# Moving the rows of maxima, a query split and two stack fills to other queues and other places in a one-core decoder layer

## The reference

```python
x = x + self_attention(layernorm(x))          # 16 heads of 8, rotary, causal
x = x + cross_attention(layernorm(x), ctx)    # 16 heads of 8, keys and values from ctx, + b_proj
x = x + moe(layernorm(x))                     # mean over tokens -> 8 experts, best 2, 128 -> 512 -> 128, gelu
```

## Time and profile before

| | |
|---|---|
| runs of the kernel before | 199.74, 200.00, 201.43 us; median 200.0 |
| the profiled execution | 200.95 us; its span 199.2 us |
| mean granted TensorE clock | 0.947 of full |
| PE busy | 166.8 us (84%) |
| DVE busy | 140.7 us (71%) |
| ACT busy | 104.8 us (53%) |
| POOL busy | 52.3 us (26%) |
| DMA | 19.05 MB, mean 96 GB/s |

### The profile page before, as it was taken

One profiled execution on the slowest core, in us unless ns is written; L12 is line 12 of the kernel. 1 busy time (PEld: TensorE's weight loads), 2 busy tenths in 40 slices (PEclk: granted clock), 3 DMA queues, 4 the chain that ended last, 5 costly groups with the idle time before them and its releaser, 6 DMA issues.

```text
span 199.2 us, 4411 instructions
## 1 busy us (share of the span) xinstructions
PE 166.8 (84%) x1500; PEld 116.1 (58%) x1508; DVE 140.7 (71%) x545; ACT 104.8 (53%) x222; POOL 52.3 (26%) x103
## 2 busy tenths in 40 slices
PE   0686195699599979989998998998998899799994
PEld 0343184485466755755764655654665556598984
DVE  2789299897347899799799889888968346525020
ACT  2132021257147656566566666766676657793451
POOL 7810005668800070030030030010115107126050
PEclk9999669589769999999999999999999999999999
DMA  5817660058227503322321321300340350170720
GB/s 150 238 35 175 164 173 18 3 148 184 70 82 196 184 25 104 110 69 58 109 82 49 98 95 35 90 0 3 113 130 3 100 143 0 17 224 26 229 66 26
DMA packets 23842, 19.05 MB, mean 96 GB/s; under 512 B 2364, under 2 KB 21820, under 8 KB 23100
## 3 DMA queue, kind: packets, MB, share of 16 engines
q1 hardware_dynamic: 22908, 17.79, 31.9%
q10 hardware_dynamic: 912, 0.98, 2.0%
HBM read 12.54 MB, written 2.49 MB: 75 GB/s over the span
## 4 chain that ended last, share of the span: by engine, by line
PE 50%; DVE 19%; DMA 15%; SPq 5%; issue 4%; POOL 3%; ACT 2%; POOLq 0%; DVEq 0%; ACTq 0%
PE psV L914 11%; PE psB L893 9%; PE psA L868 8%; DMA stackQ<-maxT 6%; DMA stackQ<-scratch 4%; DVE masked L623 4%; PE psA L958 4%; PE psM L923 3%; PE psA L975 3%; DMA stackK<-hid 3%; PE psV L975 3%; PE psM L933 3%; DVE stats L554 2%; DVE negmax L629 2%; SPq L402 2%
## 5 line engine op out<-in xcount | busy, mean ns | idle before, releaser
L753 ACT ACTIVATE E<-psB 128x512 f32<-128x512 f32 x112 | 62.3, 595 | 37.3 <-PE psB L893 15.7
L868 PE MATMUL psA<-stackK,stackQ 72*128 72x256 bf16 (+1 forms) x256 | 44.4, 277 | 11.8 <-DMA stackK<-hid 5.5
L893 PE MATMUL psB<-stackQ,stackK 74*128 74x256 bf16 (+1 forms) x256 | 42.2, 264 | 4.6 <-DMA stackQ<-maxT 3.8
L623 DVE CUSTOM_DVE_ANT_0 masked<-psA,row_mask 128x128 bf16<-128x128 f32 (+1 forms) x128 | 36.8, 352 | 11.8 <-PE psA L868 11.7
L629 DVE TENSOR_REDUCE negmax<-psA 128x2 f32<-128x512 f32 x64 | 39.7, 677 | 0.0
L868 PEld LDWEIGHTS psA<-stackK,stackQ 72*128 72x128 bf16 x256 | 23.0, 105 | 21.5 <-DMA stackQ<-scratch 8.6
L914 PE MATMUL psV<-E,V 128*9 128x256 f32 (+1 forms) x512 | 30.9, 359 | 0.2 <-ACT E L753 0.2
L893 PEld LDWEIGHTS psB<-stackQ,stackK 74*128 74x128 bf16 x256 | 22.0, 100 | 12.5 <-DMA stackQ<-maxT 5.6
L468 POOL TENSOR_SCALAR rstd<-mv 128x2 f32<-128x2 f32 x12 | 2.8, 236 | 89.1 <-DVE mv L558 88.9
L914 PEld LDWEIGHTS psV<-E,V 128*9 128x9 f32 x512 | 11.0, 90 | 14.4 <-issue 7.9
L761 ACT ACTIVATE oT<-psV 128x256 f32<-128x256 f32 x32 | 12.3, 384 | 7.9 <-PE psV L914 7.2
(11 more groups left out here) (111 smaller groups left out, 247.0 us busy)
## 6 DMA issues: line engine op xcount, KB each, us to landing
stackK<-scratch SPq DMA_DIRECT2D x18, 192.0 KB
stackQ<-hid SPq DMA_DIRECT2D x36, 64.0 KB
w1s<-w_dram SPq DMA_DIRECT2D x8, 258.0 KB, 2.8
w2s<-w_dram SPq DMA_DIRECT2D x8, 256.0 KB, 3.7
stackQ<-scratch SPq DMA_DIRECT2D x3, 576.0 KB
stackK<-hid SPq DMA_DIRECT2D x18, 64.0 KB
scratch<-hid SPq DMA_DIRECT2D x4, 192.0 KB, 3.7
scratch<-parts_ctx SPq DMA_DIRECT2D x4, 192.0 KB, 4.7
```

The source lines that it names most:

```text
L623: last = dve.tensor_tensor_reduce(out=masked[:, bank, i * keys:(i + 1) * keys], in0=scores[:, i, 0:keys], in1=row_mask[:, S - keys:S], sca ...
L753: act.activation(dst, psB[:, bank].rearrange("p (h q) -> p h q", h=dst.shape[1]), ACT.Exp, scale=SCALE).then_inc(b_taken, 1)
L868: last = pe.matmul(psA[:, bank, i * keys:(i + 1) * keys], stackQ[0:ROWS, b, h, t * P:(t + 1) * P], stackK[0:ROWS, b, h, 0:keys], start=Tru ...
L893: last = pe.matmul(psB[:, bank, i * n:(i + 1) * n], stackK[:, b, h, t * P:(t + 1) * P], stackQ[:, b, h, q0:S], start=(s == 1 or i == 0), s ...
```

## The change

Four edits in one.

1. The step max_rows is split into three. max_turn (PE's transpose) and row_out (the two DMAs) stand behind the units of half 8j+8, max_rows (DVE) stands ahead of them: DVE takes the maxima before the two new units of scores. The DMAs are issued by ACT instead of SP; ACT first waits for DVE's second instruction. Only for job 0 do the three stay together, behind half 7.
2. In q_cross ACT copies the product from PSUM into a new tile qc of two buffers, and POOL splits it from there, ahead of its addition of the bias (line 495). DVE has nothing left of this step.
3. stack_write and stack_read of batches 2 and 3 become one step for the keys (last argument 1) and one for the queries (0). For batch 2: keys written behind half 6, queries behind 9, keys read behind 9, queries behind 10 (before: both written behind 9, both read behind 10). For batch 3: 13, 14, 14, 15 (before: 14, and the read behind 17).
4. The scratch output of the masked maxima has two buffers instead of three, and its wait is for DVE's own unit before last.

```diff
+    put(7, "max_turn", 0, 0)
     put(7, "max_rows", 0, 0)
+    put(7, "row_out", 0, 0)
...
-    put(9, "stack_write", 0, 2)
-    put(10, "stack_read", 0, 2)
-    put(14, "stack_write", 0, 3)
+    put(6, "stack_write", 0, 2, 1)
+    put(9, "stack_write", 0, 2, 0)
+    put(9, "stack_read", 0, 2, 1)
+    put(10, "stack_read", 0, 2, 0)
+    put(13, "stack_write", 0, 3, 1)
+    put(14, "stack_write", 0, 3, 0)
+    put(14, "stack_read", 0, 3, 1)
+    put(15, "stack_read", 0, 3, 0)
...
         if j > 0:
-            put(n + 2 * NG, "max_rows", s, b)
-        if j == 1:
-            put(n + 2 * NG + 1, "stack_read", 0, 3)
+            row_of[n + 2 * NG] = (s, b)
...
+        if half in row_of:
+            order.append(("max_rows", *row_of[half]))
         order += [step for _, step in sorted(units, key=lambda unit: unit[0])]
+        if half in row_of:
+            order += [("max_turn", *row_of[half]), ("row_out", *row_of[half])]
...
# SP
-                if kind == "stack_write" and s == 0:
-                    sp.wait_ge(parts_k_self[b], NPART)
-                    write_parts(0, b, 1, parts[:, b, 1], scr_k_self[b])
-                    sp.wait_ge(parts_q_self[b], NPART)
-                    write_parts(0, b, 0, parts[:, b, 0], scr_q_self[b])
-                if kind == "stack_read" and s == 0:
-                    sp.wait_ge(scr_k_self[b], 16)
-                    read_k(s, b)
-                    sp.wait_ge(scr_q_self[b], 16)
-                    read_q(s, b)
+                if kind == "stack_write":
+                    which = st["g"]
+                    sp.wait_ge((parts_q_self[b], parts_k_self[b])[which], NPART)
+                    write_parts(s, b, which, parts[:, b, which], (scr_q_self[b], scr_k_self[b])[which])
+                if kind == "stack_read":
+                    which = st["g"]
+                    sp.wait_ge((scr_q_self[b], scr_k_self[b])[which], 16)
+                    if which == 1:
+                        read_k(s, b)
+                    else:
+                        read_q(s, b)
...
-                if kind == "max_rows":
-                    sp.wait_ge(misc_taken[st["misc"][0][0]], st["misc"][0][1])
-                    for i in range(2):
-                        sp.dma_start(stackQ[MAXROW + i:MAXROW + i + 1, b].rearrange("o h (t q) -> o (h t) q", t=NT),
-                                     maxT[:, b, i, :]).then_inc(maxrow_in[b], 16)
...
# POOL
                 if kind == "q_cross":
+                    bank, k = misc[0]
+                    pool.wait_ge(misc_taken[bank], k)
+                    split(qc[:, b % 2], parts[:, b, 0], parts_q[b])
...
# DVE
-                if kind == "q_cross":
-                    bank, k = misc[0]
-                    dve.wait_ge(misc_full[bank], k)
-                    qq, dst = rot[:, b % 2, 0, 0], parts[:, b, 0]
-                    dve.tensor_copy(dst[:, 0], psM[:, bank, 0:S]).then_inc(parts_q[b], 1)
-                    dve.wait_ge(parts_q[b], 1)
-                    dve.tensor_tensor(qq, psM[:, bank, 0:S], dst[:, 0], ALU.subtract).then_inc(misc_taken[bank], 1)
-                    dve.wait_ge(misc_taken[bank], k)
-                    dve.tensor_copy(dst[:, 1], qq).then_inc(parts_q[b], 1)
-                    dve.wait_ge(parts_q[b], 2)
-                    dve.tensor_tensor(dst[:, 2], qq, dst[:, 1], ALU.subtract).then_inc(parts_q[b], 1)
...
-                        if unit >= NA:
-                            dve.wait_ge(a_taken, unit - NA + 1)
+                        if unit >= 2:
+                            dve.wait_ge(a_taken, unit - 1)
...
# ACT
+                if kind == "row_out":
+                    bank, k = use[("max_turn", s, b)][0]
+                    act.wait_ge(misc_taken[bank], k)
+                    for i in range(2):
+                        act.dma_start(stackQ[MAXROW + i:MAXROW + i + 1, b].rearrange("o h (t q) -> o (h t) q", t=NT),
+                                      maxT[:, b, i, :]).then_inc(maxrow_in[b], 16)
...
+                if kind == "q_cross":
+                    bank, k = misc[0]
+                    act.wait_ge(misc_full[bank], k)
+                    if b >= 2:
+                        act.wait_ge(parts_q[b - 2], NPART)
+                    act.activation(qc[:, b % 2], psM[:, bank, 0:S], ACT.Copy).then_inc(misc_taken[bank], 1)
```

More of the change, by code:

```diff
@@ L72, in plan @@
 def plan():
-    extra = {}
+    extra, row_of = {}, {}
     def put(half, *step):
@@ L161, in plan @@
     uses = {"ln_turn": 1, "v_self": 1, "ctx_turn": 1, "k_cross": 1, "v_cross": 1, "q_cross": 1,
-            "max_rows": 1, "o_turn": 2, "o_back": 1, "o_proj": 1, "route": 1}
+            "max_turn": 1, "o_turn": 2, "o_back": 1, "o_proj": 1, "route": 1}
     count, total, steps = [0, 0], 0, []
@@ L226, in build @@
         row_mask = sb("row_mask", [P, S])
-        masked = sb("masked", [P, NA, 2 * S], BF16)
+        masked = sb("masked", [P, 2, 2 * S], BF16)
         mask16T = sb("mask16T", [P, GH, P], BF16)
@@ L239, in build @@
         kc = sb("kc", [P, NB, S])
+        qc = sb("qc", [P, 2, S])
         hid = sb("hid", [P, NHID, NC, S])
@@ L619, in _ @@
                             dve.wait_ge(row_mask_set, 1)
-                        if unit >= NA:
-                            dve.wait_ge(a_taken, unit - NA + 1)
+                        if unit >= 2:
+                            dve.wait_ge(a_taken, unit - 1)
                         for i in range(nh):
-                            last = dve.tensor_tensor_reduce(out=masked[:, bank, i * keys:(i + 1) * keys], in0=scores[:, i, 0:keys],
+                            last = dve.tensor_tensor_reduce(out=masked[:, unit % 2, i * keys:(i + 1) * keys], in0=scores[:, i, 0:keys],
                                                             in1=row_mask[:, S - keys:S], scale=-1.0, scalar=LARGEST,
@@ L870, in _ @@
                     last.then_inc(a_full, 1)
-                if kind == "max_rows":
+                if kind == "max_turn":
                     pe.wait_ge(a_taken, a_units_until(job))
```

## The result

| | before | after |
|---|---|---|
| median of 11 runs | 200.27 us (199.4 to 203.2) | 203.74 us (201.7 to 205.3) |
| ratio | | 1.0138, interval 1.0087 to 1.019 |
| profiled execution, span | 200.95, 199.2 us | 202.06, 200.3 us |
| mean granted clock in it | 0.947 | 0.940 |

The kernel became 1.4% slower, clear of noise; the forecast was 194.7 us, 2.6% faster. Both spans are taken from single executions, and executions of one kernel differ here by how long TensorE's clock stood at its half level: the mean clock c of a span s gives 2(1-c)s, 21 us in the profile before, 24 us after, and 24 to 31 us over the 11 runs after. In 24 later runs of the kernel before it was 14 to 31 us, median 20.6, and each us of it cost 0.46 us of time (a fitted line).

The account below looks back on a forecast made before the run. PE, 84% busy, was taken as the bound, with gains from its waits. Terms -5.3 +1.0 -1.3 = -5.6, 0.3 given back for fills: -5.3 us, so 194.7 us from 200.0; 8-in-10 range 192.0 to 199.0.

Parts of the forecast that it names:

- Part 1: Batch 2's stack: reads start 2.4 us earlier, PE's 2.3 us stall and the half clock behind it go, 5.3 us gained.
- Part 2: Job 1's row DMAs meeting batch 3's earlier reads: 2 us extra delay, 1.0 us PE stall, bounds 0 and 2.6.
- Part 3: Rows of maxima, six times: DVE takes them earlier, ACT issues them; row stalls shrink, new waits come, sum -1.3 us.
- part 4: q_cross: DVE loses 1.6 us in each of four jobs, ACT and POOL take the work; gain nothing.
- PE does not wait for DVE there: At DVE's four q_cross instructions, 89.84 to 91.48: reason why removing 1.6 us per job would gain nothing.
- ACT's side: ACT issuing two row DMAs, priced 1.20 us: cost nothing by 0.7 us; at 2.7 us PE would lose 0.8 per job.
- that rival: ACT becomes the bound: row_out holds ACT, psB stays taken, 4 us; 198.6 us, or 204 without Part 1 (chance 0.06).
- the second one: Job 1's maxima wait behind pieces of batch 3's reads: 2.6 us stall instead of 1.0, 196 to 198 us, chance 0.15.
- The first: Batch 2's reads are DMA-bound, or only the stall shrinks and half clock stays: 198 to 200.5 us, chance 0.13.
- The third: DVE, rid of 1.6 us, causes no new psA wait, row stalls all go: another 2 to 3 us, 191.5 to 192.5, chance 0.08.

Follow-up runs that it names:

- g5: The kernel of g4 run again with more rounds, beside c1; ratio to the kernel before 0.986 (0.978 to 0.993).
- g4: The kernel of a2, but only batch 3's query read waits for job 1's rows, its key reads go ahead; ratio to the kernel before 0.981 (0.973 to 0.990).
- b3: Kernel before with only the maxima in front on VectorE and row DMAs on ScalarE, stack steps at their old places; ratio 1.012 (1.001 to 1.024).
- b1: Kernel before with only the separate, earlier stack writes and reads of batches 2 and 3; ratio 1.028 (1.020 to 1.036).
- a2: Changed kernel, but SP waits until job 1's row DMAs have landed before reading batch 3; ratio to the kernel before 0.977 (0.972 to 0.982).
- g1: The kernel of a2 with row DMAs on SP and batch 3's reads behind half 17; ratio to the kernel before 0.972 (0.965 to 0.978).
- c1: The kernel of g4 with row DMAs on SP and batch 3's query read behind half 17; ratio to the kernel before 0.995 (0.991 to 0.998).
- a1: Changed kernel with both reads of batch 3's stacks back behind half 17; ratio to the kernel before 0.999 (0.994 to 1.005).
- a3: Changed kernel with the row DMAs issued by SP at the same place in the list; ratio to the kernel before 1.011 (1.004 to 1.018).
- g3: The kernel of a2 with the cross query split back on VectorE, reading PSUM; ratio to the kernel before 0.981 (0.975 to 0.987).
- b2: Kernel before with only the query split moved to ScalarE and GpSimd, masked scratch in two buffers; no ratio, median 205.8 against 199.9 us.
- g2: The kernel of a2 with VectorE's maxima and the row DMAs back behind the half, still on ScalarE; no ratio, median 221.1 against 201.3 us.

## Why the prediction was wrong

**Part 1 was right.** The transposes of jobs 0 and 1 lie 13.74 us apart instead of 17.02. The rest of the 5.3 us would have come behind it: g5, with 0.28 us of stall, needs 13.78 us from job 1 to job 2, the kernel before 15.61. Together 31.94 us from job 0's transpose to the first residual add became 28.4 in g4 with its stall of 1.6, so 5.2 less without it, against 5.3 forecast. The part named two causes, edit 3 and SP freed of the maxima. Either will do: b3 has the gain without edit 3 (13.93), b1 most of it with edit 3 alone (14.69).

**Part 2 was the step that failed.** The sum had 2 us of extra flight for the rows of job 1 and 1.0 us of stall, with 2.6 as its upper end. Measured were 5.5 us of extra flight (7.33 against 1.85) and 4.80 of stall, outside the bound. PE wanted the rows at 54.95, as counted; the landing was wrong. No row stands behind the bound of 2.6: with the 8.65 us that the part itself names, rows sent at 52.2 land at 60.85, and the stall is 5.9. The row that I named as the nearest one for a DMA in traffic, 8.65 us for the query read, was the right size, and I took the other end, since the rows are small and on another queue. What was issued close around them decides instead:

| reads of batch 3 around the second row DMA | its flight, us | stall, us |
|---|---|---|
| held back (a2, ScalarE; g1, SP) | 2.98; 2.94 | 0.61; 0.84 |
| keys ahead, the first by 5.2 us (g5, ScalarE) | 2.65 | 0.28 |
| keys ahead, the first by 2.4 and 2.7 us (g4, ScalarE; c1, SP) | 3.98; 4.16 | 1.61; 3.12 |
| two of three key reads ahead, the rest just behind (b3, a1, ScalarE) | 4.34; 4.67 | 1.96; 2.29 |
| keys and queries ahead (after, ScalarE) | 7.33 | 4.80 |
| keys and queries ahead (a3, b1, SP) | 6.49; 7.91 | 4.39; 6.81 |

In the changed kernel the read of the queries was issued only 0.18 us ahead of the second row DMA (52.19 and 52.37).

The Trainium skill, "DMA: Bandwidth & Descriptors", section "Queues, rings and completion order", has each DMA engine take turns between queues packet by packet. The runs show the sharing (q10's packets among q1's above), and little profit from a queue of one's own: 7.33 us on ScalarE's, 6.49 and 7.91 on SP's. Counted from the first read of batch 3, the rows landed after 9.75 us on ScalarE's queue and after 11.1 (a3) and 11.4 (b1) on SP's, where they were also issued 2.2 and 1.1 us later in that count; a profit of about a microsecond is not excluded. The section "Issuing engines are not separate DMA queues" of the same page, that a second issuer saves only issue time, fits c1 beside g4: 1.2 us earlier issue, 0.2 us of flight.

**The clock was left out of Part 2.** I counted the half clock as saved behind the one stall, and not as lost behind the other. From job 1 to job 2 the distance less the stall is 13.5 us at full clock: 13.78-0.28, 15.11-1.61, 15.47-1.96, 15.80-2.29. With a stall of 3 us and more it is 17.2, 15.3, 17.5 and 17.3 (c1, a3, after, b1): another 2 to 4 us. In these four profiles the clock fell during the stall, for 7 to 14 us, and in none of the others in that stretch. So 4.8 us of stall cost 8.8. With it the account closes: +0.65 up to job 0, -5.4 by part 1 (17.02 to 13.74, and 15.61 to 13.5), +8.8 for the rows of job 1, -3.0 behind job 2 give +1.05 of the 1.1 us. The length of a stall alone does not decide it: the kernel before had the half clock right behind its 2.31 us, a1 did not behind 2.29.

**Part 3 had its size right; part 4's "nothing" failed as well.** Forecast were -1.3 us for the rows and nothing for DVE's 1.6 us per job. Measured are -3.0 us together. The six distances from the first residual add to the seventh sum to 94.65 us in the kernel before, 93.39 in b3 (edit 1 alone) and 91.70 in the changed kernel. So edit 1 alone brought -1.26, close to the -1.3, though not spread as forecast: -0.32, -0.06, -0.03, -0.01, -0.48, -0.36 for jobs 2 to 7, against -0.4, four times -0.15 and -0.3. Edit 2 on top of it brought another -1.69, all in the four distances that hold a query split (-0.32, -0.49, -0.57, -0.30). The steps that part 3 names are there: DVE takes the maxima at 88.61, right behind ln_stats, the rows leave at 89.20, and PE's wait for the first unit grew from 0.35 to 0.84 (0.95 forecast):
```profile
88.61 0.25 DVE L634 CAST maxT<-psM 32x128 bf16<-32x128 f32 x1
...
89.09 1.27 DVE L627 TENSOR_REDUCE negmax<-psA 128x2 f32<-128x512 f32 x2
89.20 1.15 ACTq L729 DMA_DIRECT2D stackQ<-maxT  x2
89.82 0.39 PE L878 MATMUL psA<-stackK,stackQ 72*128 72x256 bf16 x2 [0.84 <-DVE negmax L627]
```
In the second and third distance the four combinations are: neither edit 15.61 and 15.67; edit 1 without 2 15.55 and 15.64 (b3, g3); edit 2 without 1 15.51 (b2, in the one of its distances that is clear of other stalls); both 15.06 and 15.07. Without edit 2 what PE wins at the rows is given back a few units later, because DVE is then behind (the chain of g3, the two waits of b3). Without edit 1 PE stands for the rows whatever DVE has to do. My sentence "PE does not wait for DVE there" was true of the kernel before, where PE stood for the rows at that moment, and not of the kernel with edit 1.

**ACT's side** went as forecast where it was forecast: two issues cost 1.15 us, and the 1.34 us price did not come. What was not seen is g2: ACT's cover hangs on DVE's place, not on the price of an issue. The 198.6 us of that rival were also added up wrongly: its 4 us take the place of part 3's -1.3, so with part 1 in place they give about 199.9.

**The rivals.** It was the second one, the maxima of job 1 late, at nearly twice its price in stall, and doubled by the clock. The first (the landing does not move) fell with part 1. The third (rows pay in full) named the right cause, DVE rid of 1.6 us, but not its way: another 1.7 us came where it had 2 to 3, and the new psA wait that it ruled out was there (0.84).

## What to carry to other kernels

A queue that waits paces what stands behind it: when a wait is taken out of it, look up where the next large transfers go, and what small, urgent transfer they will meet. If there is one, tie the large ones to its landing by a semaphore (a2); a later place in the list did not do it here (a1). Then look at the next small transfer too, since the large ones now meet that one (a2, job 2). And two removals on a path that changes engines have to be priced together: in the second and third distance each was worth 0.1 us or less, and both 0.5 to 0.6.

## What the runs showed that was not expected

A transfer of 8 KB needed 6.5 to 7.9 us with 1.1 MB of reads issued shortly before it, on either of the two queues, against 1.8 to 2.0 us in all eight jobs of the kernel before and 2.9 to 3.0 with these reads held back (a2, g1). The time of one and the same kernel spread by 9 us (a1: 196.3 to 205.1), most of it in step with how long the clock was at 1.2 GHz (14 to 31 us of the span).
